# Loads with 16384 B rows: four samples per tile, 32-row matmuls in four row groups

## The chip, the cores and the metric

The kernel runs on one core of one Trainium2 chip. The metric is the device time of one execution in microseconds, the median of several. The core has TensorE (PE) for matmuls, VectorE (DVE), ScalarE (ACT), GpSimd (POOL), SyncE (SP), which here issues nearly all transfers, and 16 DMA engines.

## The reference

```python
B, C, D, T, N_SUBJECTS = (128, 128, 128, 1024, 8)
# x (B, C, T), subjects (B,) int32 in 0..7, weights (N_SUBJECTS, C, D), all values float32
w = weights[subjects]
out = jnp.einsum('bct,bcd->bdt', x, w)
return x + out
```

Each of 128 samples is a 128 x 1024 matrix (512 KB). It is multiplied by one of eight 128 x 128 matrices, the one its subject number picks, and the sample itself is added. 67.1 MB are read and 67.1 MB written.

## The kernel before, in words

The residual addition is folded into the weights: out = (W + I) transposed, times x. A tile is two samples, and there are 64 tiles in 8 turns of 8 slots (`TILES_PER_TURN`). `x_rows` views x so that one row of 8192 B holds channels 2q and 2q+1 of a sample, one row per partition: sample g of a tile lies in partitions 64g to 64g+63. `x_ring` and `out_ring` have 8 slots of 1 MB each. The weights are loaded twice (L63), once into each half of the partitions of `table`, in rows of 1024 B.

Each engine runs its own program; semaphores join them. All loops of a turn are written out (`go_round`); the first turn stands apart because it has fewer waits.

- SP (L60 to L84) issues the two weight loads, then eight x loads (L65). Then, for each tile, it waits until DVE and ACT have drained it (L71, L72), issues its store (L73) and the load of the tile eight further on into the same slot (L77). Everything goes through one queue, in this order.
- POOL (L86 to L119) makes a unit matrix in the right arrangement (`unit`, L93), waits for the table, and then for each sample reads the subject number into a register (L105) and adds the unit matrix to the picked weights (L112), which gives `selected`, four buffers. The add permutes the output channels too, so that even and odd ones come to lie in different halves. It runs up to four tiles ahead of PE (L109).
- PE (L121 to L148) waits for x, for the selected weights and for a free pair of PSUM buffers (L128 to L132), and makes 8 matmuls per tile (L137): two halves of the times (`banks`, 512 columns each), two channels per partition (`e`, accumulated), two samples (`g`), each over 64 rows. A matmul of this type is recorded as two MATMULs and two LDWEIGHTS.
- DVE (L158) and ACT (L178) each copy half of a tile from PSUM into `out_ring`, in two copies of 64 partitions x 1024, after the product is ready and after the store of eight tiles before has left the slot. ACT also loads the subject numbers (L168).

## Time and profile before

| | us |
|---|---|
| median of 3 runs | 330.95 (330.91 to 331.18) |
| the profiled execution's own time | 331.55 |
| its span, first to last instruction | 329.2 |
| mean DMA rate over the span | 411 GB/s, 135.33 MB in 19495 packets |

The time of an execution is a little longer than its span. Busy time and the tenths of the page tell how full an engine is, not whether anything waits for it; the windows give the same by stage together with the DMA rate. In a row of the timeline, several instructions of the same kind are joined, with their count behind an x. PEclk and the granted clock are TensorE's clock as a share of 2.4 GHz. The first columns of times are microseconds from the start of the span.

### The profile page before, as it was taken

The page shows a single profiled execution, that of the slowest core. Times are in us where ns is not written, and L with a number is a line of the kernel's source. Part 1 is how long each engine was busy: PE and PEld are TensorE (multiplying, and loading weights), DVE is VectorE, ACT ScalarE, POOL GpSimd, SP SyncE. Part 2 cuts the span into 40 slices and gives each one's busy share as a digit, 9 for nine tenths or more (in the row PEclk, how much of TensorE's full clock was granted, in tenths as well). Part 3 has the DMA queues.
Part 4 walks back from the last instruction along what each step waited for, and adds up shares of the span by engine and source line. Part 5 has one row for each costly group of instructions (what it writes and reads, how often), then busy time and mean ns, then how long its engine had stood idle before and what let it go on. Part 6 is the DMA issues. An engine that isn't in the chain of part 4 may idle for free.

```text
span 329.2 us, 4043 instructions
## 1 busy us (share of the span) xinstructions
PE 236.5 (72%) x1024; PEld 107.3 (33%) x1024; DVE 156.3 (47%) x128; ACT 129.9 (39%) x129; POOL 95.1 (29%) x136
## 2 busy tenths in 40 slices
PE   0599999877677687686686786776776876866800
PEld 0244444333233233233233242332332332332300
DVE  0057767645535535435445445345355354454420
ACT  1045656534424424424334334334244244344320
POOL 1634434422323313223223223223232233230000
PEclk9999999999999999999999999999999999999975
DMA  7999999999999999999999999999999999999992
GB/s 148 409 426 419 427 422 428 429 423 426 427 426 428 428 427 426 426 427 427 429 429 424 428 426 426 428 429 426 425 427 425 428 430 426 427 425 427 427 430 101
DMA packets 19495, 135.33 MB, mean 411 GB/s; under 512 B 2081, under 2 KB 3106, under 8 KB 3106
## 3 DMA queue, kind: packets, MB, share of 16 engines
q1 hardware_dynamic: 19488, 135.27, 98.5%
q8 instruction: 2, 0.03, 0.0%
q14 instruction: 3, 0.02, 0.0%
q10 hardware_dynamic: 2, 0.00, 0.0%
HBM read 68.16 MB, written 67.11 MB: 411 GB/s over the span
## 4 chain that ended last, share of the span: by engine, by line
PE 65%; DVE 15%; DMA 9%; ACT 4%; issue 2%; DVEq 1%; POOLq 0%; SPq 0%; POOL 0%; ACTq 0%
PE products L137 65%; DVE out_ring L158 15%; DMA x_ring<-x 6%; ACT out_ring L178 4%; DMA table<-weights 2%; DVEq L34 1%; POOLq L105 0%; POOL selected L112 0%; SPq L63 0%; SPq L73 0%; ACTq L176 0%; POOLq L112 0%; SPq L77 0%; DVEq L163 0%; POOLq L97 0%
## 5 line engine op out<-in xcount | busy, mean ns | idle before, releaser
L137 PE MATMUL products<-x_ring,selected 64*128 64x512 f32 x1024 | 236.5, 604 | 76.5 <-DVE out_ring L158 48.2
L158 DVE COPY out_ring<-products 64x1024 f32<-64x1024 f32 x128 | 156.3, 1221 | 159.2 <-PE products L137 157.2
L178 ACT COPY out_ring<-products 64x1024 f32<-64x1024 f32 x128 | 128.6, 1005 | 183.7 <-PE products L137 182.1
L137 PEld LDWEIGHTS products<-x_ring,selected 64*128 64x128 f32 x1024 | 107.3, 189 | 204.8 <-issue 107.5
L112 POOL TENSOR_TENSOR selected<-table,unit 64x256 f32<-64x256 f32 x128 | 93.7, 732 | 199.4 <-PE products L137 153.3
L178 ACT ACT_TABLE_LOAD x1 | 1.3, 1283 | 1.4 <-PEq L192 1.4
L93 POOL TENSOR_SCALAR_AFFINE_SELECT unit<-ones 64x256 f32<-64x256 f32 x2 | 0.8, 412 | 0.1
L88 POOL MEMSET ones<- 128x256 f32 x1 | 0.3, 311 | 0.3 <-POOLq L192 0.3
L192 POOL MEMSET const-float32-0.0<- 128x1 f32 x1 | 0.1, 99 | 0.1
L192 POOL MEMSET const-float32-1.0<- 128x1 f32 x1 | 0.1, 98 | 0.0
L192 POOL MEMSET const-bfloat16-1.0<- 128x1 bf16 x1 | 0.1, 98 | 0.0
L192 POOL MEMSET const-uint8-127<- 128x1 uint8 x1 | 0.1, 98 | 0.0
L192 POOL BASE_LOAD x1 | 0.0, 17 | 0.2 <-issue 0.2
## 6 DMA issues: line engine op xcount, KB each, us to landing
x_ring<-x SPq DMA_DIRECT2D x64, 1024.0 KB, 26.9
out<-out_ring SPq DMA_DIRECT2D x64, 1024.0 KB, 26.5
table<-weights SPq DMA_DIRECT2D x2, 512.0 KB, 6.5
subject_row<-subjects ACTq DMA_DIRECT2D x1, 0.5 KB
```

The source lines that it names most:

```text
L34: with ExitStack() as ctx:
L88: nc.gpsimd.memset(ones[:], 1.0).then_inc(ones_ready, 1)
L93: nc.gpsimd.affine_select(unit[part, :], ones[part, :], [[128, 2], [-128, 2], [-1, HALF]], ALU.is_equal, 0.0, base=0, channel_multiplier=1 ...
L112: nc.gpsimd.tensor_tensor(selected[part, k, :].rearrange("p (e b m) -> p e b m", e=2, b=2), picked, unit[part, :].rearrange("p (e b m) -> ...
L137: last = nc.tensor.matmul(products[:, b, g, n * BANK:(n + 1) * BANK], selected[part, k, e * mixed:(e + 1) * mixed], x_ring[part, s, e * ti ...
L158: nc.vector.tensor_copy(out_ring[0:HALF, s, b * times:(b + 1) * times], products[b * HALF:(b + 1) * HALF, s % PSUM_BUFS, 0, :]).then_inc(e ...
L178: nc.scalar.copy(out_ring[HALF:channels, s, b * times:(b + 1) * times], products[b * HALF:(b + 1) * HALF, s % PSUM_BUFS, 1, :]).then_inc(o ...
L192: nc = bacc.Bacc("TRN2", target_bir_lowering=False, num_devices=1)
```

## The change

The tile becomes four samples, 32 tiles in 8 turns of 4 slots; x is viewed with four channels in a row of 16384 B (`GROUP`), sample j in partitions 32j to 32j+31. A load is one transfer of 2 MB. The output view stays at 8192 B rows: a tile is stored with two transfers of 1 MB, both issued after the whole tile is drained. The weights are loaded once, in rows of 512 B over 128 partitions (`loaded`). DVE adds the unit matrix to them once; eight matmuls against 0/1 matrices (`spread`, made by POOL) distribute the rows to the four row groups; DVE and ACT copy the eight results from PSUM into `table`, permuting the columns. POOL's work per sample is then a plain copy of 32 partitions x 512 elements, with two buffers instead of four. PE makes 32 matmuls over 32 rows per tile, in four row groups, each into a bank of its own; PSUM is handed over by halves of the times (4 banks each) and no longer by tiles. The counters `product_ready`, `even_drained` and `odd_drained` start at positive values, and so POOL and PE need no separate first turn.

The diff, cut to its core (declarations of semaphores left out; ACT's drain loop is changed as DVE's is):

```diff
--- before.py
+++ after.py
...
-TILES_PER_TURN = 8
-PSUM_BUFS = 2
-SELECT_BUFS = 4
+SLOTS = 4
+SELECT_BUFS = 2
 BANK = 512
 DMA = 16
+GROUP = 4
+QUARTER = 32
 HALF = 64
+
+DRAINED_FREE = 4
+PRODUCT_FREE = 2 * SELECT_BUFS
...
-    row = 2 * times
-    tiles = samples // 2
-    turns = tiles // TILES_PER_TURN
+    row = GROUP * times
+    pair_row = 2 * times
+    tiles = samples // GROUP
+    turns = tiles // SLOTS
     banks = times // BANK
-    wide = 2 * mixed
...
-    x_rows = x.rearrange("b (q e) t -> (b q) (e t)", e=2)
+    x_rows = x.rearrange("b (q e) t -> (b q) (e t)", e=GROUP)
     out_rows = out.rearrange("b (q e) t -> (b q) (e t)", e=2)
-    w_rows = weights.rearrange("n (q e) d -> q n (e d)", e=2)
...
-        x_ring = ctx.enter_context(nc.sbuf_tensor("x_ring", [channels, TILES_PER_TURN, row], F32))
-        out_ring = ctx.enter_context(nc.sbuf_tensor("out_ring", [channels, TILES_PER_TURN, row], F32))
+        x_ring = ctx.enter_context(nc.sbuf_tensor("x_ring", [channels, SLOTS, row], F32))
+        out_ring = ctx.enter_context(nc.sbuf_tensor("out_ring", [channels, 2 * SLOTS, pair_row], F32))
+        loaded = ctx.enter_context(nc.sbuf_tensor("loaded", [channels, n_subjects, mixed], F32))
+
-        products = ctx.enter_context(nc.psum_tensor("products", [mixed, PSUM_BUFS, 2, times], F32))
+
+        products = ctx.enter_context(nc.psum_tensor("products", [mixed, banks, GROUP, BANK], F32))
...
-            for g in range(2):
-                sp.dma_start(table[g * HALF:(g + 1) * HALF], w_rows).then_inc(table_loaded, DMA)
-            for s in range(TILES_PER_TURN):
+            sp.dma_start(loaded[:], weights.rearrange("n c d -> c n d")).then_inc(weights_loaded, DMA)
+            for s in range(SLOTS):
                 sp.dma_start(x_ring[:, s], x_rows[s * channels:(s + 1) * channels, :]).then_inc(x_loaded[s], DMA)
 
             def go_round(turn, last=False):
-                for s in range(TILES_PER_TURN):
-                    tile = turn * TILES_PER_TURN + s
-
-                    sp.wait_ge(even_drained, 2 * tile + 2)
-                    sp.wait_ge(odd_drained, 2 * tile + 2)
-                    sp.dma_start(out_rows[bass.ds(tile * channels, channels), :],
-                                 out_ring[:, s]).then_inc(stored[s], DMA)
+                for s in range(SLOTS):
+                    tile = turn * SLOTS + s
+
+                    sp.wait_ge(even_drained, DRAINED_FREE + 4 * tile + 4)
+                    sp.wait_ge(odd_drained, DRAINED_FREE + 4 * tile + 4)
+                    for h in range(2):
+                        sp.dma_start(out_rows[bass.ds((2 * tile + h) * channels, channels), :],
+                                     out_ring[:, 2 * s + h]).then_inc(stored[2 * s + h], DMA)
                     if not last:
 
-                        sp.dma_start(x_ring[:, s], x_rows[bass.ds((tile + TILES_PER_TURN) * channels, channels), :]
+                        sp.dma_start(x_ring[:, s], x_rows[bass.ds((tile + SLOTS) * channels, channels), :]
                                      ).then_inc(x_loaded[s], DMA)
...
-            for g in range(2):
-                part = slice(g * HALF, (g + 1) * HALF)
-
-                nc.gpsimd.affine_select(unit[part, :], ones[part, :], [[128, 2], [-128, 2], [-1, HALF]],
-                                        ALU.is_equal, 0.0, base=0, channel_multiplier=1).then_inc(unit_ready, 1)
-            pool.wait_ge(unit_ready, 2)
+
+            nc.gpsimd.affine_select(unit[:], ones[:, :mixed], [[-1, mixed]],
+                                    ALU.is_equal, 0.0, base=0, channel_multiplier=1).then_inc(unit_ready, 1)
+
+            nc.gpsimd.affine_select(spread[:], ones[:], [[-1, GROUP], [0, GROUP], [-GROUP, QUARTER]],
+                                    ALU.is_equal, 0.0, base=0, channel_multiplier=1).then_inc(spread_ready, 1)
             pool.wait_ge(subjects_loaded, DMA)
-            pool.wait_ge(table_loaded, 2 * DMA)
-
-            def go_round(turn, first=False):
-                for s in range(TILES_PER_TURN):
+            pool.wait_ge(table_ready, GROUP)
+
+            with pool.Fori(0, turns) as turn:
+                for s in range(SLOTS):
                     k = s % SELECT_BUFS
-                    tile = turn * TILES_PER_TURN + s
-                    for g in range(2):
-                        part = slice(g * HALF, (g + 1) * HALF)
-                        subject = pool.value_load(subject_row[0:1, bass.ds(2 * tile + g, 1)],
+                    tile = turn * SLOTS + s
+                    for j in range(GROUP):
+                        part = slice(j * QUARTER, (j + 1) * QUARTER)
+                        subject = pool.value_load(subject_row[0:1, bass.ds(GROUP * tile + j, 1)],
                                                   min_val=0, max_val=n_subjects - 1)
-                        if g == 0 and (not first or s >= SELECT_BUFS):
-
-                            pool.wait_ge(product_ready, tile - SELECT_BUFS + 1)
-                        picked = table[part, bass.ds(subject, 1), :].rearrange(
-                            "p n (e m b) -> p (n e) b m", e=2, b=2)
-                        nc.gpsimd.tensor_tensor(
-                            selected[part, k, :].rearrange("p (e b m) -> p e b m", e=2, b=2), picked,
-                            unit[part, :].rearrange("p (e b m) -> p e b m", e=2, b=2),
-                            ALU.add).then_inc(weights_selected, 1)
-
-            go_round(0, first=True)
-            with pool.Fori(1, turns) as turn:
-                go_round(turn)
+                        if j == 0:
+
+                            pool.wait_ge(product_ready, PRODUCT_FREE + 2 * (tile - SELECT_BUFS) + 2)
+                        nc.gpsimd.tensor_copy(selected[part, k:k + 1, :],
+                                              table[part, bass.ds(subject, 1), :]).then_inc(weights_selected, 1)
...
-            def go_round(turn, first=False):
-                for s in range(TILES_PER_TURN):
-                    tile = turn * TILES_PER_TURN + s
-                    k, b = s % SELECT_BUFS, s % PSUM_BUFS
+            pe.sem_inc(product_ready, PRODUCT_FREE)
+            pe.wait_ge(spread_ready, 1)
+            pe.wait_ge(unit_added, 1)
+            for e in range(GROUP):
+                for n in range(banks):
+                    last = nc.tensor.matmul(products[:, n, e, :], spread[:, e * channels:(e + 1) * channels],
+                                            loaded[:].rearrange("c n d -> c (n d)")[:, n * BANK:(n + 1) * BANK],
+                                            start=True, stop=True)
+                last.then_inc(weights_spread, 1)
+
+            with pe.Fori(0, turns) as turn:
+                for s in range(SLOTS):
+                    tile = turn * SLOTS + s
+                    k = s % SELECT_BUFS
                     pe.wait_ge(x_loaded[s], turn * DMA + DMA)
-                    pe.wait_ge(weights_selected, 2 * tile + 2)
-                    if not first or s >= PSUM_BUFS:
-
-                        pe.wait_ge(even_drained, 2 * (tile - PSUM_BUFS) + 2)
-                        pe.wait_ge(odd_drained, 2 * (tile - PSUM_BUFS) + 2)
+                    pe.wait_ge(weights_selected, GROUP * tile + GROUP)
                     for n in range(banks):
-                        for e in range(2):
-                            for g in range(2):
-                                part = slice(g * HALF, (g + 1) * HALF)
-                                last = nc.tensor.matmul(
-                                    products[:, b, g, n * BANK:(n + 1) * BANK],
-                                    selected[part, k, e * mixed:(e + 1) * mixed],
-                                    x_ring[part, s, e * times + n * BANK:e * times + (n + 1) * BANK],
-                                    start=(e == 0), stop=(e == 1))
-                    last.then_inc(product_ready, 1)
-
-            go_round(0, first=True)
-            with pe.Fori(1, turns) as turn:
-                go_round(turn)
+
+                        pe.wait_ge(even_drained, DRAINED_FREE + 4 * (tile - 1) + 2 * n + 2)
+                        pe.wait_ge(odd_drained, DRAINED_FREE + 4 * (tile - 1) + 2 * n + 2)
+                        for e in range(GROUP):
+                            for j in range(GROUP):
+                                part = slice(j * QUARTER, (j + 1) * QUARTER)
+                                at = e * times + n * BANK
+                                last = nc.tensor.matmul(products[:, n, 2 * (j % 2) + j // 2, :],
+                                                        selected[part, k, e * mixed:(e + 1) * mixed],
+                                                        x_ring[part, s, at:at + BANK],
+                                                        start=(e == 0), stop=(e == GROUP - 1))
+                        last.then_inc(product_ready, 1)
...
+            dve.sem_inc(even_drained, DRAINED_FREE)
+            dve.wait_ge(unit_ready, 1)
+            dve.wait_ge(weights_loaded, DMA)
+            nc.vector.tensor_tensor(loaded[:], loaded[:], unit[:].unsqueeze(1).to_broadcast([channels, n_subjects, mixed]),
+                                    ALU.add).then_inc(unit_added, 1)
+            for e in (0, 2):
+                dve.wait_ge(weights_spread, e + 1)
+                for n in range(banks):
+                    half = n_subjects // banks
+                    copied = nc.vector.tensor_copy(
+                        table[:, n * half:(n + 1) * half, e * mixed:(e + 1) * mixed].rearrange("p n (b m) -> p n m b", b=2),
+                        products[:, n, e, :].rearrange("p (n m b) -> p n m b", n=half, b=2))
+                copied.then_inc(table_ready, 1)
...
-                for s in range(TILES_PER_TURN):
-                    tile = turn * TILES_PER_TURN + s
-                    dve.wait_ge(product_ready, tile + 1)
-                    if not first:
-
-                        dve.wait_ge(stored[s], turn * DMA)
-                    for b in range(2):
-                        nc.vector.tensor_copy(out_ring[0:HALF, s, b * times:(b + 1) * times],
-                                              products[b * HALF:(b + 1) * HALF, s % PSUM_BUFS, 0, :]
-                                              ).then_inc(even_drained, 1)
+                for s in range(SLOTS):
+                    tile = turn * SLOTS + s
+                    for n in range(banks):
+                        dve.wait_ge(product_ready, PRODUCT_FREE + 2 * tile + n + 1)
+                        if not first and n == 0:
+
+                            dve.wait_ge(stored[2 * s], turn * DMA)
+                            dve.wait_ge(stored[2 * s + 1], turn * DMA)
+                        for b in range(2):
+                            at = b * times + n * BANK
+                            nc.vector.tensor_copy(out_ring[0:HALF, 2 * s:2 * s + 2, at:at + BANK],
+                                                  products[b * HALF:(b + 1) * HALF, n, 0:2, :]
+                                                  ).then_inc(even_drained, 1)
...
+            act.sem_inc(odd_drained, DRAINED_FREE)
+            for e in (1, 3):
+                act.wait_ge(weights_spread, e + 1)
+                for n in range(banks):
+                    half = n_subjects // banks
+                    copied = nc.scalar.copy(
+                        table[:, n * half:(n + 1) * half, e * mixed:(e + 1) * mixed].rearrange("p n (b m) -> p n m b", b=2),
+                        products[:, n, e, :].rearrange("p (n m b) -> p n m b", n=half, b=2))
+                copied.then_inc(table_ready, 1)
...
```

## Rows read from the trace of the kernel before

**Rows 1.** The page: busy time and instruction counts, and two lines of 40 slices.
```profile
PE 236.5 (72%) x1024; PEld 107.3 (33%) x1024; DVE 156.3 (47%) x128; ACT 129.9 (39%) x129; POOL 95.1 (29%) x136
DMA  7999999999999999999999999999999999999992
```
**Rows 2.** Windows: stretch, length, busy time and count of each engine, PEclk, DMA share, GB/s.
```profile
3.40:5.60 2.20, 0.00 (x0) 0.00 (x0) 0.00 (x0) 0.00 (x0) 0.00 (x0) 1.00 1.08 254
5.60:7.00 1.40, 0.00 (x0) 0.00 (x0) 0.00 (x0) 0.00 (x0) 0.00 (x0) 1.00 1.13 229
9.00:23.00 14.00, 11.10 (x40) 5.29 (x42) 3.68 (x4) 3.25 (x4) 8.37 (x12) 1.00 1.01 421
23.00:60.00 37.00, 36.61 (x172) 17.18 (x171) 26.14 (x22) 21.37 (x22) 15.47 (x22) 1.00 1.01 426
60.00:285.00 225.00, 167.11 (x724) 75.27 (x726) 111.11 (x92) 91.66 (x92) 66.55 (x92) 1.00 1.01 427
285.00:322.00 37.00, 21.64 (x96) 9.60 (x92) 15.39 (x13) 12.36 (x13) 3.32 (x5) 0.94 1.01 427
322.50:328.30 5.80, 0.00 (x0) 0.00 (x0) 0.00 (x0) 0.00 (x0) 0.00 (x0) 0.50 0.10 42
```
**Rows 3.** The chain that ended last, in order of time: start, length, what.
```profile
1.66 7.51 DMA table<-weights
11.90 23.54 PE products L137 x96
...
119.65 3.72 PE products L137 x16
...
309.30 3.70 PE products L137 x16
```
**Rows 4.** Timeline of SP's queue, head and plateau; last, time to landing (page).
```profile
0.87 1.41 SPq L63 DMA_DIRECT2D table<-weights  x2
...
20.95 0.37 SPq L73 DMA_DIRECT2D out<-out_ring  x1
21.53 0.36 SPq L77 DMA_DIRECT2D x_ring<-x  x1
...
154.61 1.88 SPq L73 DMA_DIRECT2D out<-out_ring  x1
...
160.16 5.34 SPq L77 DMA_DIRECT2D x_ring<-x  x1
...
x_ring<-x SPq DMA_DIRECT2D x64, 1024.0 KB, 26.9
```
**Rows 5.** Timeline of the head: start, length, engine, line, operation; idle before it.
```profile
10.22 6.38 POOL L112 TENSOR_TENSOR selected<-table,unit 64x256 f32<-64x256 f32 x8 [8.07 <-issue]
...
12.89 0.37 PEld L137 LDWEIGHTS products<-x_ring,selected 64*128 64x128 f32 x2 [0.48 <-issue]
13.74 0.37 PEld L137 LDWEIGHTS products<-x_ring,selected 64*128 64x128 f32 x2 [0.49 <-issue]
...
17.66 0.20 PEld L137 LDWEIGHTS products<-x_ring,selected 64*128 64x128 f32 x2 [0.23 <-issue]
18.09 0.20 PEld L137 LDWEIGHTS products<-x_ring,selected 64*128 64x128 f32 x2 [0.23 <-issue]
```
**Rows 6.** The page's groups: busy, mean ns of one; idle before, and what ended it.
```profile
L158 DVE COPY out_ring<-products 64x1024 f32<-64x1024 f32 x128 | 156.3, 1221 | 159.2 <-PE products L137 157.2
L178 ACT COPY out_ring<-products 64x1024 f32<-64x1024 f32 x128 | 128.6, 1005 | 183.7 <-PE products L137 182.1
...
L112 POOL TENSOR_TENSOR selected<-table,unit 64x256 f32<-64x256 f32 x128 | 93.7, 732 | 199.4 <-PE products L137 153.3
...
L93 POOL TENSOR_SCALAR_AFFINE_SELECT unit<-ones 64x256 f32<-64x256 f32 x2 | 0.8, 412 | 0.1
L88 POOL MEMSET ones<- 128x256 f32 x1 | 0.3, 311 | 0.3 <-POOLq L192 0.3
```
**Rows 7.** Windows at the end: the granted clock after the last matmul (columns as above).
```profile
313.10:317.60 4.50, 0.00 (x0) 0.00 (x0) 2.37 (x2) 1.93 (x2) 0.00 (x0) 1.00 1.03 435
...
317.70:322.00 4.30, 0.00 (x0) 0.00 (x0) 0.00 (x0) 0.00 (x0) 0.00 (x0) 0.50 1.01 429
```

More of the change, by code:

```diff
@@ L82, in _ @@
             go_round(turns - 1, last=True)
-            for s in range(TILES_PER_TURN):
+            for s in range(2 * SLOTS):
                 sp.wait_ge(stored[s], turns * DMA)
@@ L168, in _ @@
             act.dma_start(subject_row[:], subjects.rearrange("(a b) -> a b", a=1)).then_inc(subjects_loaded, DMA)
-            def go_round(turn, first=False):
-                for s in range(TILES_PER_TURN):
-                    tile = turn * TILES_PER_TURN + s
-                    act.wait_ge(product_ready, tile + 1)
-                    if not first:
-                        act.wait_ge(stored[s], turn * DMA)
-                    for b in range(2):
-                        nc.scalar.copy(out_ring[HALF:channels, s, b * times:(b + 1) * times],
-                                       products[b * HALF:(b + 1) * HALF, s % PSUM_BUFS, 1, :]
-                                       ).then_inc(odd_drained, 1)
+            act.sem_inc(odd_drained, DRAINED_FREE)
[7 more added lines that the diff above has]
+                copied.then_inc(table_ready, 1)
+            def go_round(turn, first=False):
+                for s in range(SLOTS):
+                    tile = turn * SLOTS + s
+                    for n in range(banks):
+                        act.wait_ge(product_ready, PRODUCT_FREE + 2 * tile + n + 1)
+                        if not first and n == 0:
+                            act.wait_ge(stored[2 * s], turn * DMA)
+                            act.wait_ge(stored[2 * s + 1], turn * DMA)
+                        for b in range(2):
+                            at = b * times + n * BANK
+                            nc.scalar.copy(out_ring[HALF:channels, 2 * s:2 * s + 2, at:at + BANK],
+                                           products[b * HALF:(b + 1) * HALF, n, 2:4, :]
+                                           ).then_inc(odd_drained, 1)
             go_round(0, first=True)
```

19 lines of the change are left out of this document (12 added, 7 removed).

## The prediction

> **What bounds the kernel now.** I read the page's tenths first, then the windows by stage, then the chain, then both ends. The busy shares point at nothing: TensorE (PE) 72%, VectorE (DVE) 47%, ScalarE (ACT) 39%, GpSimd (POOL) 29% [rows 1]. The DMA engines are busy in every slice but the first and the last, and the windows give 426 to 427 GB/s from 23 us to 322 us [rows 2]. The chain of waits nevertheless calls itself 65% matmul, because it hands each tile's start to PE. Its matmul steps take 3.72 us each but follow one another every 4.99 us in the plateau ((309.30 - 119.65) over 38 tiles) [rows 3]. A tile of two samples moves 2.10 MB, which at 427 GB/s takes 4.91 us. So PE has work for three quarters of a tile and waits for data for the rest. The kernel is a DMA pipe: time = when the pipe starts + bytes / 427 + time in which it stands empty + tail. Any edit counts only through those terms.
>
> Three details of the ends matter. The pipe starts slowly: from 3.4 to 8 us it moves 229 to 254 GB/s while the two table loads, each into 64 partitions, pass; the second lands at 9.17 us [rows 2, 3]. It then never empties: the eight first loads (8.39 MB, 19.6 us at 427) reach to about 27.5 us, and the first store is issued at 20.95 us [rows 4]. And it ends unevenly: the rate holds to 322 us, then 42 GB/s with a DMA share of 0.10 trickle to 328.3 [rows 2]: one or two of 16 engines finish late, 6.7 us between the end of the plateau (322.5) and the end of the span (329.2).
>
> **The steady part after the change.** Bytes are nearly the same: 67.1 MB each way; the weights are loaded once (0.52 MB) instead of twice. Loads have half the rows at twice the size; stores are unchanged. The trace shows no 16384 B row, so I bound what that does: nothing, as bytes at 427, up to 1.6 us gained; on the losing side I allow the head's pace, where loads alone ran at 421 against 427 [rows 2], 1.4% of half the bytes, 2.2 us lost. I take 1 us gained, near nothing, because a plateau equal in every window looks like a rate of bytes.
> The Trainium skill (DMA: Bandwidth & Descriptors, "Why small descriptors are slow") puts a fixed overhead of about 3 cycles on each packet inside a DMA engine. Loads lose 256 packets per engine, so by that page 256 x 3 / 0.85 GHz = 0.9 us would be gained, an estimate; no view here separates it.
>
> PE must stay under the pipe. A tile is now four samples: 4.19 MB, 9.82 us of pipe. It has 32 matmuls, recorded as 64 (the trace has 1024 for 512 written ones, [rows 1]). Now two row groups run at once: weight loads come two together every 0.43 us, 17.66 then 18.09 [rows 5], so 16 records take 8 x 0.43 = 3.44 us. The trace has no 32-row matmul. With four at once a tile is 16 slots x 0.43 = 6.9 us, under 9.82; with pairs only it is 13.8 us. I take four, since the two groups show no mutual delay. Drains keep their number and shape: 64 x 1024 elements, 128 on each of two engines, 1.22 and 1.00 us [rows 6], so 4.9 us per tile on DVE. POOL copies 32 x 512 four times a tile, at most 1.5 us each (twice the 732 ns of the add over 256, [rows 6]), 6 us. All are under 9.82, so these edits cost nothing while the DMA queue covers them. The cover is 39.3 us of ring (4 slots x 9.82) less about 9.5 of matmul and drain; stores and loads queued behind a landing hold over 20 us.
>
> **The head, step by step.** This is where the new work is exposed. The pipe has 8.39 MB of x to load at first and then nothing until the first store, which waits for a whole four-sample tile behind a longer preparation. Times are from the span's start.
> 1. Weights: issue at 0.87, bulk from 3.4 as before [rows 2, 4]. 0.52 MB into 128 partitions at 427 takes 1.2 us, and landing follows about 1.1 later: 5.8. Upper bound: 9.2 as now, if 512 B rows cost per row what 1024 B rows did. I take 5.8, because 229 GB/s is about half of 427 and the present loads reach half of the partitions.
> 2. Unit added on DVE over 1024 elements: 1.2 us, like the copy of 1024 (1.22, [rows 6]); bounds 1.0 (ACT's copy) to 2.5 (POOL's add scaled). 7.1.
> 3. Spreading: 8 matmuls of 128 rows, 16 records, one after another. The clock decides: the first records come every 0.86 us (12.89, 13.74), later ones every 0.43, the change being at about 17.2, 5.3 us after the first matmul at 11.90 [rows 3, 5]; these are the levels 1.2 and 2.4 GHz. So about 6.3 records slow (5.4 us), 9.7 fast (4.2 us): 9.6 us, from 7.2 to 16.8. Bounds 6.9 (all fast) and 13.8 (all slow).
> 4. Last two copies of 512 elements on ACT: 0.6 each, over half of 1.00, and the wait: 18.1. The other copies lie beside the matmuls.
> 5. POOL: today 1.04 us from landing (9.18) to its first add (10.22) [rows 3, 5], then 0.8 per add. The copy of 512 lies between 0.5 (memset 311 ns for 256 elements) and 1.5; I take 0.7 plus 0.1, near the one-input select (412 ns for 256) [rows 6]. First at 19.1, four done at 22.3; bounds 20.8 and 25.1.
> 6. Tile 0 on PE: at 2.4 GHz 6.9 + 0.16. But PE has stood idle for 5.5 us (16.8 to 22.3). At the end of the trace the last matmul ends at 313.0 and the granted clock is 1.00 until 317.6 and 0.50 after it, 4.6 us later [rows 3, 7]. So I expect 1.2 GHz again and 9.75 us: 32.05. If it stays: 29.35.
> 7. Last two drains 2.5, SP 0.2, first bytes 1.8 after issue (0.87 to between 2.4 and 3.4): the pipe resumes at 36.4 (33.7 at the kept clock).
> Loads have ended at 4.8 + 19.6 = 24.5 (the earlier start of the weights gains 3.2 us here and is spent waiting). So the pipe is empty for about 12 us (9). Later tiles do not reopen the gap: tile 0 releases 9.8 us of stores and loads, and tile 1 is drained 6.9 us after it.
> SP's waits for a whole tile also hold the load behind the stores: nothing else is queued on SP, and only the pipe waits for it. DVE's and ACT's two waits for stores are covered by the queue. The start values of the counters and the dropped first turns remove no busy time.
>
> **The tail.** Before it is 6.7 us. The engine that sets landings needs 4.99 us per tile where the mean needs 4.91, 3.7 us over 46 tiles of the plateau, in the stage where SP's issues take 1.9 to 5.3 us instead of 0.35 [rows 3, 4]: SP is blocked by a full queue. After the change at most nine transfers are in flight rather than eleven (26.9 us to landing / 2.45), so I expect less blocking and a tail of 3.5 us; bounds 3.0 and 6.7, or 10 if what slows that engine goes with matmul instructions, which double.
>
> **Sum.** 36.4 + 125.8 MB / 427 (294.7) - 1.0 + 3.5 = 333.6 of span. The profiled execution took 331.55 against a span of 329.2: 2.35 around it, giving 335.95; that execution lies 0.6 above the median of the runs, 330.95, so 335.3.
>
> **Rivals.**
> (a) Same mechanism with the clock kept: 2.7 us less, 332.6. For it: the idle time exceeds the observed 4.6 by only one. Against: the sign of that one.
> (b) Four row groups don't run at once. Pairs only: 22 + 32 x 13.8 + 7 = 471 us. A partial loss matters in the steady part from 0.61 us per slot (9.82 us per tile). For it: no row shows 32 rows. Against: two groups overlap without loss.
> The Trainium skill (TensorE: Matmul & The Clock Gate, "Why this matters for your kernels") gives 3.07x for four 32-row tiles. By it a slot is 4 x 0.43 / 3.07 = 0.56 us, a tile 9.0, still under the pipe; only tile 0 would be longer, about 2 us, 337.4. The trace's pairs agree with a full 2x and say nothing of four.
> (c) Faster: the clock is at 2.4 GHz early in the spreading (2.7 less) and kept (2.7 less), and the slow engine's loss vanishes (tail 3.0): 335.3 - 5.4 - 0.5 = 329.4. It decides where the gap shrinks below about 8 us. For: the earlier weights. Against: 6.9 us of spreading at best, before any selection.
> (d) The change does nothing measurable: gap, earlier start and a short tail cancel, 330.3 to 331.6.
>
> **How the numbers follow.** Forecast with the low clock, 333.8 to 341: 0.60. (a), 331.6 to 333.8: 0.17. (b): 0.08. (c): 0.08. (d): 0.07. About 0.2% is what a measurement of this kernel can tell from no change. Slower is 0.60 + 0.17 + 0.08 = 0.85. The range leaves out (b) and (c): low 331.0; high is 335.3 + 3.2 (tail as before) + 2.5 (part of late weights or a slow selection) = 341.0.
>
> **What would show it.** DMA tenths fall in the fourth and fifth slice (24 to 36 us); the first store is issued near 34.6; weights land near 5.8; 16 spread records take near 9.6 us; 64 records of a steady tile take 6.9 us; tile 0's slots are 0.86 us at first; the plateau is 427 to 429 GB/s; SP issues take 0.35 us. The prediction fails if the pipe doesn't empty, if 16 KB rows change the plateau by over 1%, or if a tile on PE needs over 9.8 us.

## The result, and the profile after

| | before | changed |
|---|---|---|
| median, us | 330.94 (330.91 to 331.18, 4 runs) | 339.49 (339.05 to 340.63, 4 runs) |
| profiled execution, us | 331.55 | 339.55 |
| its span, us | 329.2 | 337.8 |
| first store issued, us | 20.95 | 34.72 |

The ratio is 1.0261, with an interval of 1.0249 to 1.0273: the change makes the kernel 2.6% slower. The forecast was 335.3 us in a range of 331.0 to 341.0. Medians, here and below, leave out executions in a slower state of the chip, of which there was one (changed_warm_early, 340.93 us).

The page of the changed kernel answers rows 1: busy times, the granted clock, the DMA tenths and the DMA rate in 40 slices of 8.4 us.

```profile
PE 254.8 (75%) x2064; PEld 124.7 (37%) x2064; DVE 161.5 (48%) x133; ACT 133.8 (40%) x133; POOL 79.4 (24%) x136
...
PEclk9978999999987979899999798997999999597995
DMA  7980899999999999999999999999999999999984
GB/s 278 427 351 3 303 361 421 424 436 419 423 426 426 430 428 431 425 433 430 421 430 430 430 433 432 429 417 432 429 429 438 431 421 426 428 429 431 425 351 201
```

The busy shares have hardly moved. What has is the DMA row: its fourth slice is zero, and the rate climbs back over three slices (303, 361, 421) before it is at the level of rows 2. The windows put numbers on each stage (columns as in rows 2; an x with a number counts instructions):

```profile
24.00:24.80 0.80, 0.80 (x8) 0.37 (x4) 0.00 (x0) 0.00 (x0) 0.65 (x2) 0.50 0.00 0
25.00:35.00 10.00, 10.00 (x88) 4.82 (x84) 4.89 (x4) 4.02 (x4) 2.39 (x5) 0.87 0.01 2
35.60:48.00 12.40, 12.40 (x120) 6.04 (x116) 9.40 (x8) 7.93 (x8) 3.59 (x6) 1.00 1.00 357
60.00:285.00 225.00, 175.25 (x1472) 87.09 (x1464) 111.91 (x92) 91.99 (x92) 55.49 (x92) 0.95 1.01 428
285.00:322.00 37.00, 30.07 (x232) 14.58 (x236) 17.67 (x15) 14.64 (x15) 7.28 (x12) 0.86 1.01 428
325.50:328.30 2.80, 0.00 (x0) 0.00 (x0) 1.81 (x2) 1.38 (x2) 0.00 (x0) 0.95 0.47 199
328.30:333.00 4.70, 0.00 (x0) 0.00 (x0) 0.00 (x0) 0.00 (x0) 0.00 (x0) 0.50 1.01 420
333.00:337.80 4.80, 0.00 (x0) 0.00 (x0) 0.00 (x0) 0.00 (x0) 0.00 (x0) 0.50 0.07 31
```

From 24 to 35 us nothing flows; the pipe resumes at about 35.6. The next 12.4 us run at 357 GB/s instead of 427, which loses 12.4 x (1 - 357 / 427) = 2.0 us more. The plateau, which is the long stretch at an even rate, is at 428. At the end one engine of 16 is alone again (DMA share 0.07).

The head in the timeline of the changed kernel (start, length, engine, line):

```profile
5.37 1.23 DVE L163 TENSOR_TENSOR loaded<-loaded,unit 128x1024 f32<-128x1024 f32 x1 [5.37 <-DMA loaded<-weights]
6.75 9.00 PE L133 MATMUL products<-loaded,spread 128*128 128x512 f32 x16 [6.75 <-DVE loaded L163]
...
15.78 1.92 ACT L201 COPY table<-products 128x512 f32<-128x512 f32 x2 [1.48 <-PE products L133]
18.98 0.60 POOL L123 COPY selected<-table 32x512 f32 x1 [16.54 <-issue]
...
22.15 37.31 PE L152 MATMUL products<-x_ring,selected 32*128 32x512 f32 x320 [6.40 <-POOL selected L123]
...
32.05 2.47 DVE L185 COPY out_ring<-products 64x1024 f32<-64x1024 f32 x2 [0.96 <-PE products L152]
...
34.72 0.91 SPq L86 DMA_DIRECT2D out<-out_ring  x2
```

Read it as a relay, in which each step waits for the one above: weights, unit, spreading, copies, selection, tile 0, drain, store. (The line of tile 0 joins its 64 records with those of the next tiles; tile 0 ends at 32.05. Between the last copy, 17.70, and the first selection, 18.98, lie 1.3 us.) Before the change the relay had no unit, spreading and copies, half the selections and half of tile 0, and its store came at 20.95 us (rows 4) with loads queued until 27.5. Three windows show the clock between the spreading and the end of tile 0:

```profile
15.80:20.80 5.00, 0.00 (x0) 0.00 (x0) 0.21 (x1) 1.90 (x2) 1.48 (x3) 1.00 1.02 436
20.90:27.60 6.70, 5.45 (x28) 2.63 (x32) 0.00 (x0) 0.00 (x0) 3.27 (x6) 0.50 0.42 177
27.70:32.00 4.30, 4.30 (x44) 2.09 (x44) 2.44 (x2) 2.01 (x2) 0.00 (x0) 1.00 0.00 0
```

The clock fell to 0.50 at 20.8 us, 5.1 us after the last spreading matmul, and came back 5.5 us after tile 0 had begun. At full clock tile 0's 64 records would have taken 7.15 us, as a tile of the plateau shows; they took 9.9.

```profile
277.80 7.15 PE L152 MATMUL products<-x_ring,selected 32*128 32x512 f32 x64 [2.84 <-POOL selected L123]
```

That line also settles rival (b): 64 records of 32 rows in 7.15 us are 16 slots of 0.43 us and 0.27 us at the end; one after another they would take 64 x 0.43 = 27.5 us. So four row groups run at once.

### The profile page after: what moved, and what is told of

Same layout as the page of the kernel before. It is cut to its first block, busy times and chain, and to the rows that moved or that the text cites. A ratio compares the mean times of both kernels' runs of the same rounds, so it can differ in the third digit from the quotient of the medians.

```text
span 337.8 us, 5998 instructions
## 1 busy us (share of the span) xinstructions
PE 254.8 (75%) x2064; PEld 124.7 (37%) x2064; DVE 161.5 (48%) x133; ACT 133.8 (40%) x133; POOL 79.4 (24%) x136
## 4 chain that ended last, share of the span: by engine, by line
PE 62%; DMA 16%; issue 5%; DVE 5%; POOL 3%; POOLq 2%; ACT 1%; DVEq 1%; SPq 1%
PE products L152 60%; DMA x_ring<-x 14%; DVE out_ring L185 5%; POOL selected L123 3%; PE products L133 3%; POOLq L118 1%; DMA loaded<-weights 1%; ACT out_ring L217 1%; SPq L86 1%; DVEq L39 1%; ACT table L201 1%; POOLq L123 0%; DVE loaded L163 0%; DVEq L182 0%; DVEq L190 0%
## 5 line engine op out<-in xcount | busy, mean ns | idle before, releaser
L152 PE MATMUL products<-x_ring,selected 32*128 32x512 f32 x2048 | 245.8, 632 | 63.3 <-POOL selected L123 30.6
L152 PEld LDWEIGHTS products<-x_ring,selected 32*128 32x128 f32 x2048 | 120.9, 199 | 188.1 <-issue 120.7
L123 POOL COPY selected<-table 32x512 f32 x128 | 77.7, 607 | 228.3 <-PE products L152 170.3
L133 PE MATMUL products<-loaded,spread 128*128 128x512 f32 x16 | 9.0, 726 | 6.7 <-DVE loaded L163 6.7
L201 ACT COPY table<-products 128x512 f32<-128x512 f32 x4 | 3.9, 1068 | 11.1 <-PE products L133 11.1
L133 PEld LDWEIGHTS products<-loaded,spread 128*128 128x128 f32 x16 | 3.7, 241 | 11.2 <-issue 11.2
L169 DVE COPY table<-products 128x512 f32<-128x512 f32 x4 | 3.9, 1049 | 5.5 <-PE products L133 5.5
L163 DVE TENSOR_TENSOR loaded<-loaded,unit 128x1024 f32<-128x1024 f32 x1 | 1.2, 1226 | 5.4 <-DMA loaded<-weights 5.4
L107 POOL TENSOR_SCALAR_AFFINE_SELECT spread<-ones 128x512 f32<-128x512 f32 x1 | 0.7, 726 | 0.0
## 6 DMA issues: line engine op xcount, KB each, us to landing
out<-out_ring SPq DMA_DIRECT2D x64, 1024.0 KB, 21.9
```

The costliest lines, as they stand in the source:

```text
L107: nc.gpsimd.affine_select(spread[:], ones[:], [[-1, GROUP], [0, GROUP], [-GROUP, QUARTER]], ALU.is_equal, 0.0, base=0, channel_multiplier= ...
L123: nc.gpsimd.tensor_copy(selected[part, k:k + 1, :], table[part, bass.ds(subject, 1), :]).then_inc(weights_selected, 1)
L133: last = nc.tensor.matmul(products[:, n, e, :], spread[:, e * channels:(e + 1) * channels], loaded[:].rearrange("c n d -> c (n d)")[:, n * ...
L152: last = nc.tensor.matmul(products[:, n, 2 * (j % 2) + j // 2, :], selected[part, k, e * mixed:(e + 1) * mixed], x_ring[part, s, at:at + B ...
L163: nc.vector.tensor_tensor(loaded[:], loaded[:], unit[:].unsqueeze(1).to_broadcast([channels, n_subjects, mixed]), ALU.add).then_inc(unit_a ...
L169: copied = nc.vector.tensor_copy(table[:, n * half:(n + 1) * half, e * mixed:(e + 1) * mixed].rearrange("p n (b m) -> p n m b", b=2), prod ...
```

## The experiments

Three theories stood against each other. **Gap**: the pipe stands empty between the end of the first loads and the first store, and every microsecond of the first store counts. **Steady**: larger transfers, or longer rows, cost time in the plateau. **Slow engine**: one DMA engine loses time on its way, and the change alters how much.

### Closing the clock gap: warm_bridge

```diff
+            pe.wait_ge(table_ready, GROUP)
+            for e in range(2):
+                for n in range(banks):
+                    nc.tensor.matmul(products[:, n, e, :], spread[...], loaded[...], start=True, stop=True)
```

> The changed kernel with four more matmuls of 128 rows on TensorE (results unused, written over) between the copies into the table and tile 0, so that TensorE is idle for 2 us and 1 us instead of 6.4 us. Gap theory (the DMA pipe is empty from 24.8 us until the first store, and whatever shortens the chain to that store shortens the kernel): the granted clock stays at 1.00 through tile 0, whose 64 records take 7.15 us instead of 9.9; the first store is issued 2.75 us earlier, at about 32.0 us, and the time falls from 339.5 to 336.7 us. Rival (the larger transfers cost the time in the steady part, the head is made up for later): no change, 339.5 us, perhaps more for the added work.

Measured: 338.55 us (338.37 to 339.04), first store at 33.35. The direction is right and the size a third of what was expected. TensorE stood for 2.0 us before the bridge matmuls, and the clock fell all the same as they began; they ran at a mean clock of 0.68, took 5.4 us instead of 3.4 and pushed tile 0 from 22.15 to 23.46; tile 0 itself then ran at full clock. The first store came 1.4 us earlier and the time fell by 0.9 (in the profiled execution, the span by 1.4).

```profile
18.20:23.40 5.20, 5.20 (x8) 2.04 (x8) 0.00 (x0) 0.00 (x0) 3.11 (x6) 0.68 0.98 419
23.50:30.60 7.10, 7.10 (x69) 3.51 (x72) 2.44 (x2) 2.01 (x2) 1.65 (x3) 1.00 0.04 13
```

### The same, begun early: changed_warm_early

```diff
             pe.wait_ge(spread_ready, 1)
+            for _ in range(4):
+                nc.tensor.matmul(products[:, 1, 3, 0:256], spread[:, :channels], ones[:, 0:256], start=True, stop=True)
             pe.wait_ge(unit_added, 1)
...
+            pe.wait_ge(table_ready, GROUP)
+            for _ in range(3):
+                nc.tensor.matmul(products[:, 1, 3, 0:256], spread[:, :channels], ones[:, 0:256], start=True, stop=True)
```

> The changed kernel with four unused matmuls of 256 columns on TensorE while the weights are still being loaded (from about 2.5 us) and three more between the copies into the table and tile 0. Gap theory: the clock rises before the spreading, whose 16 records take about 6.9 us instead of 9.0, and stays up through tile 0 (7.15 instead of 9.9 us); the first store is issued near 29.9 instead of 34.7 us, the pipe is empty for about 6 us instead of 11, and the time is 334.7 us. Every microsecond of the first store's time that is won shows in the total. Rival (most of the added time is lost in the plateau or the tail): less than half of that gain, above 337 us.

Measured: 335.94 us (335.62 to 337.31), first store at 31.95. The 16 spreading records took 7.13 us, as expected; the clock fell all the same before tile 0 (0.55 from 20.6 to 24.0 us), so that tile 0 took 8.7 us and not 7.15. That is most of the 2.0 us by which the first store missed its 29.9.

```profile
7.02 7.13 PE L135 MATMUL products<-loaded,spread 128*128 128x512 f32 x16 [0.74 <-DVE loaded L168]
```

In the profiled execution the first store came 2.8 us earlier and the span was 2.5 us shorter (335.3 for 337.8); the median fell by 3.6 us. The gap theory's exchange of one for one holds within the spread of the executions; "less than half of the gain" does not.

### The table by DMA instead of TensorE: table_by_dma

```diff
-            sp.dma_start(loaded[:], weights.rearrange("n c d -> c n d")).then_inc(weights_loaded, DMA)
+            for j in range(GROUP):
+                sp.dma_start(table[j * QUARTER:(j + 1) * QUARTER], w_rows).then_inc(weights_loaded, DMA)
...
-                        nc.gpsimd.tensor_copy(selected[part, k:k + 1, :], table[...])
+                        nc.gpsimd.tensor_tensor(selected[...], picked, unit[part, :], ALU.add)
```

> The changed kernel without the spreading by TensorE: the weights are loaded four times, each into 32 partitions (rows of 2048 B), and GpSimd adds the unit matrix while it selects, as the kernel before does. Gap theory: 2.1 MB of weights at 220 to 250 GB/s land at about 13.5 us, x loads run from about 12.4 to 32 us, selection of tile 0 with four adds of about 1.4 us ends at 20.4, tile 0 at 1.2 GHz ends at 30.1, the first store is issued at 32.8 and the pipe resumes at 33.7: empty for under 2 us instead of 11, resuming 1.9 us earlier than in the changed kernel, so about 337.6 us, although the weights cost the pipe 7.6 us more. Rival (the empty stretch costs nothing, the steady part does): those 7.6 us are added, 347 us.

Measured: 337.43 us (336.68 to 338.27). The weights now hold the pipe 7.5 us longer, and the kernel is 2.1 us faster than the changed one: first store at 32.11, loads until 31.2, and then the pipe is all but empty for only 1.7 us.

```profile
3.50:12.40 8.90, 0.00 (x0) 0.00 (x0) 0.00 (x0) 0.00 (x0) 0.74 (x2) 1.00 1.08 233
...
31.20:32.90 1.70, 1.70 (x20) 0.84 (x16) 0.74 (x2) 0.30 (x2) 1.62 (x2) 1.00 0.07 19
33.00:46.00 13.00, 13.00 (x128) 6.39 (x124) 9.65 (x8) 7.92 (x8) 9.44 (x8) 1.00 1.00 362
```

Two things stand in these windows. The four loads, each into 32 partitions, run at 233 GB/s with rows of 2048 B, as rows 2 show 229 to 254 for 64 partitions and rows of 1024 B, while the changed kernel's one load into 128 partitions with rows of 512 B was down in under 3 us. A packet of 1024 B took 80 ns (median, kernel before) and one of 2048 B 161 ns, the same rate for twice the length, while one of 512 B took 27 ns. So longer rows would not have helped; of what differs between these loads, the partitions reached are left as the cause. And after the short stop the pipe again runs slowly, 362 GB/s over 13 us, 2.0 us lost. That is the same loss as after the long stop.

### Only the row size undone: rows_8k

```diff
-                        sp.dma_start(x_ring[:, s], x_rows[bass.ds((tile + SLOTS) * channels, channels), :]
-                                     ).then_inc(x_loaded[s], DMA)
+                        for h in range(2):
+                            sp.dma_start(x_ring[:, s, h * pair_row:(h + 1) * pair_row],
+                                         x_rows[bass.ds((tile + SLOTS) * channels, channels),
+                                                h * pair_row:(h + 1) * pair_row]
+                                         ).then_inc(x_loaded[s], DMA)
```

> The changed kernel with each 2 MB load issued as two transfers of 1 MB whose rows are 8192 B (the left and the right half of the 16384 B rows); everything else stays. Gap theory: rows of 16384 B are worth next to nothing, plateau 427 to 428 GB/s, first store still at 34.7 us, time 339.5 us within 1 us. Rival 1 (16384 B rows or 2 MB transfers cost time in the plateau): 331 to 336 us. Rival 2 (the DMA engine that ends last loses a fixed time per packet, so fewer packets shorten the tail): about 1 us more, 340.5 us.

Measured: 342.48 us (341.69 to 344.35), 3.0 us more than with rows of 16384 B. The steady theory falls: the long rows don't cost. The gap theory's "339.5 within 1 us" is missed too; of the three forecasts only rival 2 had the sign, at a third of the size. The run undoes two things at once, the length of the rows and the number of transfers (two of 1 MB for one of 2 MB), and can't tell which of them helps. The profiled execution was the slowest, 344.35, 4.8 over the changed kernel's; of these, 1.0 is a later first store (35.68), as spreading and tile 0 took 9.5 and 10.2 us; the plateau ran at 425 GB/s instead of 428, 1.6 us over 225 us; and the last engine ended 7.1 us after the middle one instead of 5.8. That makes 3.9; the rest is not accounted for.

```profile
60.00:285.00 225.00, 176.67 (x1444) 87.27 (x1444) 109.94 (x90) 90.46 (x90) 55.83 (x92) 0.92 1.01 425
```

### Less loaded ahead in the kernel before: before_4_slots

```diff
-TILES_PER_TURN = 8
+TILES_PER_TURN = 4
```

> The kernel before with rings of four slots instead of eight (turns of four tiles), so that only 4.2 MB are loaded ahead. Gap theory: these loads end at about 18 us, the first store is issued at 20.95 and its bytes flow at about 21.8, so the pipe is empty for 3.9 us and the time rises by as much, 334.8 us; the plateau stays at 427 GB/s. Rival (the number of transfers in flight sets the steady rate, and the head is made up for later): a changed plateau, or no change in time, 331 us.

Measured: 334.37 us (333.58 to 335.13), ratio 1.0095 (1.0077 to 1.0112). The stop is there, and so is the slow stretch behind it; the plateau is untouched.

```profile
18.10:20.90 2.80, 2.80 (x16) 1.40 (x14) 1.81 (x3) 1.38 (x3) 0.92 (x2) 1.00 0.01 3
20.90:28.00 7.10, 6.77 (x32) 2.89 (x28) 5.12 (x5) 4.25 (x5) 3.08 (x5) 1.00 1.01 321
60.00:285.00 225.00, 168.73 (x732) 76.10 (x730) 110.88 (x91) 90.96 (x91) 66.00 (x91) 1.00 1.01 427
```

With none of the change's parts in it, the kernel before loses 3.4 us when its first loads end before its first store. That is the mechanism nearly alone (the output ring is halved as well). The 2.8 us of standstill and 7.1 x (1 - 321 / 427) = 1.8 us of slow restart make 4.6. The loads landed 0.3 us earlier here and the last engine ended 4.6 us behind the middle one instead of 5.9, which leaves 3.0; the span grew by 3.7 (332.9 for 329.2), so 0.7 us is not accounted for.

### Only the weights' part: spread_pairs and pairs_warm_early

The kernel before, with the weights loaded once into 128 partitions and spread by four matmuls. The second has the clock raised beforehand.

```diff
-            for g in range(2):
-                sp.dma_start(table[g * HALF:(g + 1) * HALF], w_rows).then_inc(table_loaded, DMA)
+            sp.dma_start(loaded[:], weights.rearrange("n c d -> c n d")).then_inc(weights_loaded, DMA)
...
+            for e in range(2):
+                for n in range(2):
+                    last = nc.tensor.matmul(products[:, e, n, 0:BANK], spread[...], loaded[...], start=True, stop=True)
+                last.then_inc(weights_spread, 1)
```

> The kernel before (two samples per tile, rows of 8192 B, eight slots) with only the weights' part of the change: one load into 128 partitions, the unit matrix added by DVE, four matmuls that spread the rows to the two row groups, copies by DVE and ACT, a plain copy on GpSimd. Gap theory: x loads start near 4.9 instead of 8.1 us and end near 24.5; the spreading is half as long (8 records, about 5.5 us), the table is ready near 14, tile 0 has two selections and 16 records, and its store is issued near 22.3 us, before the loads end, so the pipe does not empty and the 3.2 us are kept: 327.7 us. Rival (spreading by TensorE is what costs, wherever it stands): above 330.9 us.

Measured: 330.17 us (329.03 to 331.45), ratio to the kernel before 0.9970 (0.9956 to 0.9984). The first store came at 26.51 us, 4.2 later than expected, after the loads' end. I had forecast the spreading and tile 0 with a clock that had risen; both ran at half clock, 6.7 us for 8 records. So the pipe stopped, and 2.4 of the 3.2 us were lost again. The rival, that spreading costs wherever it stands, falls too: the kernel is not slower, but 0.3% faster.

```profile
6.58 6.66 PE L125 MATMUL products<-loaded,spread 128*128 128x512 f32 x8 [6.58 <-DVE loaded L159]
```

> The kernel before with only the weights' part of the change (one load into 128 partitions, spreading by four matmuls), as in the run spread_pairs, with five unused matmuls of 256 columns before the weights land and three after the spreading. Spread_pairs missed its 22.3 us for the first store by 4.2 us, because spreading and tile 0 ran at half clock. Gap theory: with the clock up from the start the spreading takes 3.5 us, tile 0 3.7, the first store is issued near 21 us, before the first loads end at 24.5; the pipe never empties and keeps the 3.2 us of shorter weights: 327.7 us, faster than the kernel before (330.95). Rival (the earlier start is lost again elsewhere): 330 to 331 us.

Measured: 328.33 us (327.27 to 329.20), ratio 0.9912 (0.9893 to 0.9931), 0.9% faster than the kernel before. The spreading took 4.06 us. But tile 0 met a low clock once more, and its store came at 24.14, so that the pipe still stopped for 0.8 us (24.2 to 25.0) and paid for the restart.

```profile
6.41 4.06 PE L127 MATMUL products<-loaded,spread 128*128 128x512 f32 x8
...
14.80:21.50 6.70, 6.70 (x18) 3.07 (x20) 0.01 (x1) 0.01 (x1) 2.37 (x6) 0.55 1.02 424
24.50:25.00 0.50, 0.50 (x4) 0.21 (x2) 0.08 (x1) 0.08 (x1) 0.00 (x0) 1.00 0.00 0
26.00:32.00 6.00, 6.00 (x30) 2.88 (x28) 4.02 (x5) 3.18 (x4) 1.27 (x4) 1.00 1.00 288
```

6.0 x (1 - 288 / 427) = 2.0 us are lost after a stop of 0.8. Whether a version whose first store is issued before the loads end would keep these as well wasn't tried; the transfers alone, below, have such a slow stretch without any stop.

### Two queues for the table: before_two_queues

```diff
-            for g in range(2):
-                sp.dma_start(table[g * HALF:(g + 1) * HALF], w_rows).then_inc(table_loaded, DMA)
+            sp.dma_start(table[0:HALF], w_rows).then_inc(table_loaded, DMA)
...
+            act.dma_start(table[HALF:channels], w_rows).then_inc(other_loaded, DMA)
```

> The kernel before with the second of its two table loads issued from ScalarE's queue instead of SyncE's, so that the loads into partitions 0 to 63 and 64 to 127 run beside each other. If the 220 to 250 GB/s of the table loads come from each load reaching only half of the partitions (as the changed kernel's single load into 128 partitions, 0.52 MB from 2.0 to 4.9 us, suggests), both land at about 6.5 instead of 9.2 us, x loads start up to 2.4 us earlier and the time falls from 330.9 to 328.6 us. If the rate comes from rows of 1024 B or the number of rows, nothing changes: 330.9 us.

Measured: 331.19 us (329.73 to 331.40), ratio 0.9996 (0.9985 to 1.0007): no change. The two loads, though issued together, landed one after the other at 6.2 and 8.8 us, so the second queue did not make them run side by side. By the wording of its expectation this run would speak for the rows as the cause. But its premise failed, that the two loads would run beside each other, so it says nothing on the rows; table_by_dma and the changed kernel's load do, and they speak against them. The Trainium skill (SBUF — State Buffer, "Can I just issue two DMAs to hit both halves?") says that two such transfers serialize; this run agrees, with landings 2.6 us apart.

### Transfers alone, and what slows the last engine

Four kernels leave out the product and store x again: the first two have only the transfers, the last two one engine's instructions beside them (excerpt, shortened):

```diff
+            for tile in range(AHEAD):
+                load(tile)
+            for tile in range(tiles):
+                s = tile % SLOTS
+                sp.wait_ge(x_loaded[s], (tile // SLOTS + 1) * DMA)
+                for h in range(parts):
+                    sp.dma_start(out_rows[...], x_ring[:, s, ...]).then_inc(stored[s], DMA)
+                new = tile + AHEAD
+                if new < tiles:
...
+                    load(new)
```

> Transfers alone: every x tile of 1 MB (rows of 8192 B) is loaded and stored again from the same place, with no matmul, copy or weights, so the output is x. It shows what the slowest of the 16 DMA engines loses without any other instructions. If its loss goes with packets or bytes, the others end about 316 us and it ends 4 to 6 us later, time near 324 us; if the loss goes with instructions of the compute engines or with their table and code loads, all engines end within 1 us, time near 318 us.

> The same transfers alone with loads of 2 MB in rows of 16384 B and stores of 1 MB in rows of 8192 B, as in the changed kernel. If rows of 16384 B save a fixed time per packet (the run with 8192 B rows in the changed kernel took 3 us more), this is 1 to 3 us faster than transfers alone with 8192 B rows. If the row size is worth nothing, the two agree within 0.5 us.

> Transfers alone as in pipe_8k, beside which TensorE makes 8 matmuls of 64 rows on constant data after each load lands (the kernel before's amount). The slowest DMA engine ended 0.95 us after the middle one in pipe_8k and 5.93 after it in the kernel before. If the instruction stream of TensorE causes the loss, it is 4 us or more here; if not, about 1 us.

> Transfers alone as in pipe_8k, beside which GpSimd reads two subject numbers and makes two adds over 64 x 256 elements after each load lands (the kernel before's amount). If GpSimd's stream causes the slowest engine's loss, it ends 4 us or more after the middle one here, and about 1 us in the run with matmuls; if neither does, VectorE's and ScalarE's copies or the waits between engines remain.

Each transfer is completed by 16 engines, one by one, and the trace holds all 16 times. The table gives, for one of the last stores, how long the last engine came after the middle (eighth) one.

| kernel (one profiled execution each) | median time, us | last engine behind, us |
|---|---|---|
| pipe_8k | 321.52 | 0.95 |
| pipe_16k | 321.87 | 3.06 |
| pipe_8k_matmuls | 322.83 | 2.73 |
| pipe_8k_select | 323.01 | 2.22 |
| before | 330.94 | 5.93 |
| changed (tile 30) | 339.49 | 5.82 |
| rows_8k (tile 30) | 342.48 | 7.09 |

For pipe_8k neither time I had written (324 or 318) is met. The start holds a slow stretch that I had left out, which costs 4 x (1 - 285 / 427) = 1.3 us; the lag decides, and it is that of "no compute instructions": 0.95 us.

```profile
20.00:24.00 4.00, 0.00 (x0) 1.00 0.94 285
24.00:285.00 261.00, 0.00 (x0) 1.00 1.01 427
```

(Columns: the busy time of GpSimd, then the granted clock, DMA share and GB/s.) The DMA engines are 94% busy in that stretch: the rate falls without a stop, where the first loads end and the first stores begin to flow. All four of these runs have it (285 to 324 GB/s from 20 to 24 us), and the kernel before, with the same transition at about 27 us, has not (425 GB/s from 26 to 34 us).

Beside matmuls the lag is 1.8 us longer and beside GpSimd's selections 1.3, and both kernels are 1.3 and 1.5 us slower than pipe_8k; I had expected one of them to bring 4 us and the other nothing. But 1.4 of the matmuls' 1.8 us came in one jump, between 15 and 26 us (0.20 to 1.58), in the slow stretch; it then stood at 1.55 until 160 us, where that of the kernel before grows all the way (0.15 at 36 us, 3.4 at 163, 6.0 at 310). And pipe_16k lags by 3.06 with no compute at all. So work beside the transfers seems to bring a part of the lag, but how much, and by which engine, is not shown; VectorE's and ScalarE's parts weren't tried alone.

Pipe_16k came out on the second branch of its expectation: within 0.5 us of pipe_8k, its plateau at 428 against 427 GB/s. The 3 us between rows_8k and the changed kernel are thus shown only inside that kernel.

## Why the prediction was right, and where it was not

**Right: the pipe and its gap.** The pipe ran empty and stood for 11.7 us (23.8 to 35.5), about the 12 of step 7, and each microsecond of the first store counted. The weights' part alone, on pairs, doesn't slow the kernel (330.17 us), and the tile of four samples without the spreading still takes 337.43; so the loss comes with the larger tile, whose spreading, selection and product all stand before the first store. The head went as the steps said:

| step | forecast, us | measured, us |
|---|---|---|
| weights landed | 5.8 | 5.3 |
| spreading ends | 16.8 | 15.75 |
| last copies end | 18.1 | 17.7 |
| first selection starts, four done | 19.1, 22.3 | 18.98, 21.9 |
| tile 0 done | 32.05 | 32.0 |
| store issued | 34.6 | 34.72 |
| pipe resumes | 36.4 | 35.6 |

Step 3 was near (9.0 us for 9.6), step 4 too short (two copies of 0.96 us for 0.6 each; why they are longer is not shown), step 5 well placed (0.60 us for a copy, forecast 0.7), and step 6's decision for the low clock was right: rival (a) did not come, nor (c), nor (d). The last term of step 7 was too long: bytes flow 0.9 us after the issue, not 1.8. The 3.2 us of shorter weights were spent waiting, as forecast. That the store came within 0.1 us of its forecast is partly luck: weights 0.5 us early and spreading 0.6 us shorter made up for the copies, 0.6 us longer.

**Right: no cost in the steady part.** Four row groups run at once, the plateau is 428 GB/s, and all the PE, POOL, DVE and ACT work of a tile fits under it. The 3.07x for four 32-row tiles that the Trainium skill gives (TensorE: Matmul & The Clock Gate, "Why this matters for your kernels") would have made a tile of 9.0 us; the trace has 7.15, with 4 records in each slot of 0.43 us, so the measurement decides. The 1.0 us that the sum took off for the longer rows is about what the plateau gives: 428 for 427 is 0.7 us over 294.7.

**Missed: the restart.** Nothing in the sum stood for the 12.4 us at 357 GB/s after the pipe resumes; it is the step "the pipe resumes at 36.4, then 427 GB/s". It costs 2.0 us. It is there in every run with a stop, 1.8 to 2.0 us each where it was worked out (changed, before_4_slots, table_by_dma, pairs_warm_early), whether the stop was 11.7 us or 0.8, and absent in the kernel before (rows 2: 426 from 23 us on). But the stop is not what it needs: the transfers alone lose 1.0 to 1.3 us in such a stretch without one. In the changed kernel's 12.4 us, 35 of the 289 packets of 8192 B took over 500 ns, most of them near 606, where the plateau's take 309. What slows them is not shown.

**Missed: the tail.** I sized it at 3.5 us and it is about as before. The reason I gave was that SP's blocked issues go with the slow engine's loss. SP is indeed no longer blocked, but the loss stays:

```profile
277.68 0.87 SPq L86 DMA_DIRECT2D out<-out_ring  x2
...
278.75 0.35 SPq L90 DMA_DIRECT2D x_ring<-x  x1
```

Against 1.88 and 5.34 us (rows 4), these issues take 0.44 and 0.35, and the last engine is 5.8 us behind all the same. Pipe_8k shows the reverse, issues as long as those of the kernel before and a lag of only 0.95 us:

```profile
154.21 2.25 SPq L38 DMA_DIRECT2D x_ring<-x  x1
...
157.06 5.98 SPq L38 DMA_DIRECT2D x_ring<-x  x1
```

So the reason was wrong, and what makes the engine slow stays open. Its lag also brings a second stop: tile 31 waits for the slow engine's share of its load (landed at 317.3, the middle engine's at 311.9), so the others run out of work one by one from 325.8 us until the next stores at 328.3; the slow one completes a store every 2.44 us to the end, at 332.4, 334.9 and 337.3, and never stops. So the second stop adds nothing to the slow engine's own end.

The forecast's tail was the time from the end of the full rate to the end of the span. Counted so, it is 2.8 x (1 - 199 / 427) = 1.5 us for the second stop and 4.8 us after 333.0, together 6.3 (6.7 before). The sum is then -0.8 (resumed earlier) + 2.0 (restart) + 2.8 (tail 6.3 for 3.5) = 4.0, and 333.6 + 4.0 = 337.6 of span against 337.8 measured.

That the range reached as far as 339.49 is partly luck. Its upper end had room for the tail, which was needed, and 2.5 us for late weights or a slow selection, which did not come; the restart, for which no room was made, fell into those.

## What to carry to other kernels

When a kernel is bound by its transfers, count the bytes that can be loaded before the first result and set them against the time to that result: here 8.4 MB last 19.6 us, and a change that brings these loads forward by 3.2 us but delays the first store by 13.8 us costs 2.6%. Bigger tiles put more into that first result; the steady part does not show it. The spreading began at half clock in every run that did not raise the clock before (9.0 us, against 7.13 with it raised), so such a preparation should be costed so, or the clock raised while the transfers are still under way.

## What the runs showed of the hardware

- After a stop between the first loads and the first store, the pipe runs at 288 to 362 GB/s for 6 to 13 us instead of 427, and loses 1.8 to 2.0 us, however short the stop. Transfers alone fall to 285 to 324 GB/s for 4 us at the same transition without a stop.
- The granted clock can fall for less idle time than at the end of rows 7 (4.6 us): in warm_bridge it fell when TensorE had stood for 2.0 us, and in pairs_warm_early it stood for 2.9 us and tile 0 had a mean of 0.55. In the changed kernel, with 2.8 us idle per tile, the clock fell in some tiles of the plateau (mean 0.95; rows 2 have 1.00 with 1.3 us idle), which costs nothing there, since the pipe is the bound.
- Loads into 32 or 64 partitions ran at 229 to 254 GB/s with rows of 2048 or 1024 B; the changed kernel's 0.52 MB into 128 partitions with rows of 512 B landed 4.4 us after its issue. The Trainium skill (SBUF — State Buffer, "Door 1: The DMA port swizzle") says that 64 partitions reach no more ports than 32, and the rates of these runs agree.
- One of the 16 DMA engines ended 4.6 to 7.1 us behind the middle one in the kernels with all engines at work, and 0.95 and 3.06 us behind in the two with transfers alone.
